# Transposed probabilities in a new packing, and a landing buffer two transfers deep

## The reference

```
q = x_norm @ wq ; k, v = x_norm @ wkv          # 32 heads, 128 columns each
scores = q @ k.T * scale, masked to k <= q     # 1024 x 1024 per head
probs  = softmax(scores)
attn   = probs @ v ; x = x + attn @ wo
```

## Time and profile before

| what | value |
|---|---|
| median of three runs | 1215.86 us |
| span of the profiled execution, first to last instruction | 1215.2 us |
| TensorE matmul busy | 1186.3 us, 98% of the span, 6400 matmuls |
| VectorE busy | 863.2 us, 71% |
| ScalarE busy | 820.0 us, 67%, 1527 instructions |
| GpSimd busy | 316.7 us, 26% |
| placing (line 533) | 384 instructions, 305.6 us |
| transposing transfers | 256, median 3.3 us from issue to landing |

### The profile page before, as it was taken

The page is one execution under the profiler, slowest core; times in us unless marked ns, Lnnn a source line. Parts: engine busy times, 40 slices in busy tenths (PEclk is TensorE's granted clock), DMA queues, the critical chain, the costliest instruction groups (busy, mean ns, idle before and its releaser), DMA issues.

```text
span 1215.2 us, 20757 instructions
## 1 busy us (share of the span) xinstructions
PE 1186.3 (98%) x6400; PEld 1036.9 (85%) x6400; DVE 863.2 (71%) x1490; ACT 820.0 (67%) x1527; POOL 316.7 (26%) x281
## 2 busy tenths in 40 slices
PE   4999999999999999999999999999999999999798
PEld 3888889888888988888898988889898888988677
DVE  7566776777677677667767676776767677777873
ACT  2576767676676667667667757766776776767753
POOL 3323122313322231322223132223313222230300
PEclk9999999999999999999999999999999999999999
DMA  3354435444443545444345444434453453454401
GB/s 121 70 112 103 98 79 108 93 102 98 97 104 73 106 99 105 98 95 104 71 101 109 98 95 99 104 78 94 106 106 86 101 110 81 87 105 96 102 1 70
DMA packets 354549, 114.34 MB, mean 94 GB/s; under 512 B 305888, under 2 KB 348384, under 8 KB 354528
## 3 DMA queue, kind: packets, MB, share of 16 engines
q1 hardware_dynamic: 354528, 114.08, 44.4%
HBM read 36.44 MB, written 2.10 MB: 32 GB/s over the span
## 4 chain that ended last, share of the span: by engine, by line
PE 95%; DVE 2%; DMA 1%; ACT 1%; issue 0%; SPq 0%; DVEq 0%; ACTq 0%
PE psC L781 61%; PE psC L833 17%; PE psS L781 16%; DMA pt<-p 1%; DVE p L709 0%; DMA res<-in_L_attn_hidden_states 0%; DVE probs L633 0%; PE psS L794 0%; ACT pT L533 0%; DVE xT L639 0%; DVE res L668 0%; ACT probs L515 0%; DVE stats L609 0%; ACT p L524 0%; DVE qkT L734 0%
## 5 line engine op out<-in xcount | busy, mean ns | idle before, releaser
L781 PE MATMUL psC<-xT,wqk 128*128 128x512 f32 x1536 | 372.2, 391 | 1.7 <-DVE xT L639 1.7
L781 PEld LDWEIGHTS psC<-xT,wqk 128*128 128x128 f32 x1536 | 286.1, 189 | 60.8 <-DVE xT L639 2.1
L533 ACT ACTIVATE pT<-pt 128x1024 fp32r<-128x1024 f16 (+3 forms) x384 | 305.6, 841 | 2.4 <-DMA pt<-p 2.4
L781 PE MATMUL psS<-qkT 128*128 128x512 f32 (+2 forms) x1152 | 245.5, 342 | 1.1 <-ACT probs L515 1.1
L709 DVE SCALAR_TENSOR_TENSOR p<-probs,p 128x128 f16<-128x128 f32 (+7 forms) x256 | 221.2, 869 | 16.1 <-ACT p L524 16.0
L703 DVE TENSOR_TENSOR psS<-psS,mask 128x128 f32<-128x128 f32 x256 | 75.7, 296 | 220.5 <-PE psS L781 219.9
L668 DVE SCALAR_TENSOR_TENSOR res<-psC,rinv,res 128x512 f32<-128x512 f32 x256 | 186.4, 743 | 61.4 <-PE psC L781 54.7
L833 PE MATMUL psC<-pT,v 128*128 128x512 f32 (+2 forms) x1152 | 221.2, 346 | 1.9 <-DVE res L668 1.1
L833 PEld LDWEIGHTS psC<-pT,v 128*128 128x128 f32 x1152 | 196.5, 188 | 30.4 <-DVE res L668 2.7
L781 PEld LDWEIGHTS psS<-qkT 128*128 128x128 f32 x1152 | 198.4, 189 | 27.8 <-ACT probs L515 1.6
L515 ACT ACTIVATE probs<-psS,negmax 128x128 f32<-128x128 f32 (+7 forms) x256 | 189.2, 739 | 44.3 <-DVE negmax L705 43.6
(11 more groups left out here) (55 smaller groups left out, 611.9 us busy)
## 6 DMA issues: line engine op xcount, KB each, us to landing
raw<-in_L_attn_wkv SPq DMA_DIRECT2D x64, 256.0 KB, 3.9
raw<-in_L_attn_wq SPq DMA_DIRECT2D x32, 256.0 KB, 3.1
raw<-in_L_attn_wo SPq DMA_DIRECT2D x32, 256.0 KB, 4.4
pt<-p SPq DMA_TRANSPOSE x256, 3.3
res<-in_L_attn_hidden_states SPq DMA_DIRECT2D x8, 256.0 KB, 6.0
out<-res SPq DMA_DIRECT2D x8, 256.0 KB, 2.0
raw<-in_L_ffn_k SPq DMA_DIRECT2D x3, 256.0 KB, 3.6
scl<-in_L_ffn_s SPq DMA_DIRECT2D x3, 0.5 KB, 5.1
```

Source lines behind the costliest of these rows:

```text
L533: last = nc.scalar.activation(pT[:, :, places, :], src[:, :, first_kt:first_kt + m, :], ACT.Copy, scale=1.0 / UP)
L781: last = nc.tensor.matmul(out_ap, w, x, start=(k == 0), stop=(k == len(terms) - 1))
```

## The change

The places of `pT` get a new formula, `pt16` shrinks from 26 to 15 places, placing is one instruction for every tile, and SP gets a wait. Blocks of tiles i >= 4 stand in rows of four (stride 4 from kt to kt+1); blocks of tiles i < 4 stand in the places that such rows leave unused, with stride -5. The zero block moves from place 15 to place 0.

```
 def block_at(kt, i):
-    return 7 * kt + i if kt < 4 else 13 + 3 * kt + i
-ZERO_AT = 15
-PLACES = block_at(7, 7) + 1
-def sections(i): ...
+    return 1 + 4 * kt + i - 4 if i >= 4 else 33 - 5 * kt + i
+ZERO_AT = 0
+PLACES = block_at(0, 3) + 1
+def places_of(i):
+    if i >= 4:
+        return slice(block_at(0, i), block_at(i, i) + 1, 4)
+    return slice(block_at(0, i), block_at(i, i) - 1, -5)
...
-        pt16 = sb("pt16", [P, 26, 2 * P], F16)
+        pt16 = sb("pt16", [P, 15, 2 * P], F16)
...
         def turned_blocks(n):
-            at = (0, 5, 11, 18)[n % 4]
+            at = (0, 7)[n % 2]
...
                     if step == "l":
+                        if not isinstance(g, int) or count(g, j, 8, n - 1) > 0:
+                            sp.wait_ge(placed, count(g, j, 8, n - 1))
+                            sp.sem_inc(turn_go, 1)
                         sp.wait_ge(p_lo, count(g, j, 8, n + 1))
                         sp.sem_inc(turn_go, 1)
                         sp.dma_start_transpose(turned_blocks(n), ...)
...
             def place(g, j, n):
-                for first_kt, m, places in sections(n):
-                    last = nc.scalar.activation(pT[:, :, places, :], src[:, :, first_kt:first_kt + m, :],
-                                                ACT.Copy, scale=1.0 / UP)
-                last.then_inc(placed, 1)
+                nc.scalar.activation(pT[:, :, places_of(n), :], src, ACT.Copy, scale=1.0 / UP).then_inc(placed, 1)
...
-    nc = _bacc.Bacc("TRN2", target_bir_lowering=False, num_devices=1)
+    nc = _bacc.Bacc("TRN2", target_bir_lowering=False, num_devices=1, dynamic_dma_scratch_size=1024)
```

More of the change, by code:

```diff
@@ L165, in block_at @@
 def block_at(kt, i):
-    return 7 * kt + i if kt < 4 else 13 + 3 * kt + i
-ZERO_AT = 15
-PLACES = block_at(7, 7) + 1
-def sections(i):
-    m = min(i, 3) + 1
-    out = [(0, m, slice(block_at(0, i), block_at(m - 1, i) + 1, 7))]
+    return 1 + 4 * kt + i - 4 if i >= 4 else 33 - 5 * kt + i
+ZERO_AT = 0
+PLACES = block_at(0, 3) + 1
+def places_of(i):
     if i >= 4:
-        out.append((4, i - 3, slice(block_at(4, i), block_at(i, i) + 1, 3)))
-    return out
+        return slice(block_at(0, i), block_at(i, i) + 1, 4)
+    return slice(block_at(0, i), block_at(i, i) - 1, -5)
 def build(nc, hidden, wq, wkv, wo, k0, s0, k1, s1, k2, s2, out):
```

## The result

| | median of the runs | lowest to highest |
|---|---|---|
| before | 1215.78 us | 1215.49 to 1216.01 (4 runs) |
| after | 1221.63 us | 1220.32 to 1224.62 (4 runs) |

The ratio is 1.0047, 95% interval 1.0035 to 1.0060: the changed kernel is slower by 5.9 us, where +2.5 was forecast and 1220.6 was the upper end of the range. Its profiled execution took 1222.37 us with a span of 1220.5. The run stands 1.9 us over its span here and 0.8 before; in every later comparison the kernel before has 1.8 too, and so has the change without the smaller scratch, so this difference belongs to the measuring and not to the change.

A forecast was written before the change was run, and what follows sets the result against it. TensorE was taken to bound the kernel (matmuls in flight 98% of the span). Loop 0, first group +2.0 and end of attention +0.5 gave +2.5 us, span 1217.7, plus 0.7 to the runs' median: 1218.4 us, range 1215.9 to 1220.6.

The forecast's parts named there:

- Placing in one instruction, 0: All heads: 128 fewer ScalarE instructions save 12.8 us of ScalarE's work, worth 0 behind a busy TensorE.
- places of pT, 0: TensorE's matmuls: the wider gap to the zero block costs 0, bounds -1 and +1 us.
- 280: Sign, whole kernel: placing falls to 256 instructions and about 280 us busy.
- The rival that ScalarE is the bound: Whole kernel: 12.8 us less ScalarE work releases something, 1213 us or less; chance 0.04.
- The loop, 0: 14 passes: ScalarE waits about 2.2 us per pass at c1@1, slack before s6@1 hides it; 0 us.
- First group, +2.0: First group: later transfers 3 and 4 delay chains v5 by 1.05 and v6 by 0.9 us; bounds 0 and 3.8.
- 4.9 us behind the loads: First group: transfer 3, issued behind the weight loads, takes 4.9 us to land.
- pays twice: Rival, first group: transfer 4 lands after 5.1 us, v6 is 1.8 us later, 1220.2 us; chance 0.12.
- End of attention, +0.5: End of attention: +0.2 from transfer 7 of the last head, 0.3 from GpSimd beside VectorE; bounds 0.1 and 1.
- The 0.2 for transfer 7@1: End of attention: waiting for c5@1 sends it about 0.3 us later, c7@1 in one piece gives 0.1 back.
- two regions are enough everywhere: Rival, first group: TensorE absorbs the shift, leaving +0.4, 1216.3 us, not slower; chance 0.14.
- stalling loop: Rival, loop: e4@1 is late for s6@1, each microsecond over the slack costs 14 us; chance 0.10.

The follow-up runs named there:

- layout: New places and one-instruction placing, but four landing regions, no wait and the default scratch: 1216.07 us, 1.0002 against the kernel before.
- scratch: Kernel before with only the smaller scratch of the DMA rings: 1216.14 us against 1215.72, ratio 1.0001.
- wait loop: Changed kernel with four landing regions, default scratch, and the wait in the 14 loop passes alone: 1215.76 us, 0.9998 against before.
- Loop later: The kernel of "wait loop", with transfer 1@1 also waiting for chain o1@0 in every loop pass: 1231.14 us, 1.0123 against before.
- the two with fill: Seven unread matmuls ahead of v5 in the first group, default scratch: added to the change 1220.63 us, 1.0035; added to "wait first" 1219.72 us, 1.0025.
- Loads late: Changed kernel with default scratch, the first head's four weight loads behind transfer 3 instead of transfer 2: 1218.38 us, 1.0022 against before.
- wait last: Changed kernel with four landing regions, default scratch, and the wait in the last group and end of attention alone: 1218.08 us, 1.0013 against before.
- default scratch: Changed kernel without the smaller scratch of the DMA rings: 1221.08 us, 1.0048 against before.
- two deep: Two landing regions and the wait, but old places, two instructions for tiles 4 to 7, and default scratch: 1221.14 us, 1.0048 against before.
- wait third: Changed kernel with four landing regions, default scratch, and a wait for the place of tile n-3 instead of n-2: 1216.05 us, 1.0005 against before.
- wait first: Changed kernel with four landing regions, default scratch, wait in the first group alone: 1220.57 us, 1.0034 against before; again 1218.50 us, 1.0017.

## Why the prediction was wrong, step by step

- *Placing in one instruction, 0; places of pT, 0; scratch, 0.* Right, each by itself: "layout" and "scratch" lie 0.35 and 0.42 us from before, inside their intervals. (The gap to the zero block was 9 places in chain 0 and 26 in chain 1; the prediction read only the 9.) The instruction itself was right too (1916 ns, 295.7 us in all; 280 was written as 305.6 less 128 x 0.197, which should have used the 0.1 us that two in a row overlap, 292.8). The rival that ScalarE is the bound is refuted by "layout".
- *The loop, 0.* Right: 1014.12 and 1014.13 us, and "wait loop" is at 0.9998. ScalarE waits at c1@1 as worked out (2.35 us for some 2.2), in the pass of the earlier trace rows:

```profile
647.15 0.63 ACT L532 ACTIVATE pT<-pt 128x512 fp32r<-128x512 f16 x1 [2.35 <-DMA pt<-p]
```

  The slack was put down to s6@1 with 2.3 us; in after it is 2.0, and o2@0, through qk2@2's evacuation, has one of 2.2 beside it. "Loop later" went past both. The cover is as thin as said: past it each delay costs 14 passes.
- *First group, +2.0.* The mechanism was right: SP waits, the loads and transfer 3 go later, h5@0 and v2 with them, v5 and v6 lack a bank. The term was too small. It moved transfer 3 by 2.1 us, rightly (54.3 worked out, 54.2 measured), and kept its landing at the 4.9 of the one row there was the earlier trace rows. In the eight traces where it stands in the old position it lands after 4.8 to 5.5 us, all at no cost; in the seven where it stands in the new one after 5.0 to 6.5, and v2's release passes each tenth to v5 in full. The stretch costs +2.64 in the best trace, +3.2 in the two with fill, +3.6 to +4.5 in four others, and on medians +4.4 and +1.75 in two comparisons of the same kernel, whose intervals (2.7 to 5.6 and 1.0 to 3.3) meet at about 3. The step that failed is "4.9 us behind the loads": a single landing behind 1 MB of loads was used as if it were a constant. Of after's 3.63, 1.95 was in the sum, 0.8 is the landing (5.7 for 4.9), 0.5 the way from the landing to v4's evacuation (24.7 us by the count above, 24.2 in the prediction; 0.2 of it is transfer 4, 3.5 for 3.3), and 0.4 the lower clock. I had put the long landing on transfer 4 (the rival "pays twice") where it came on transfer 3. "Loads late" shows the same from the other side: with transfer 3 ahead of the loads it goes to +0.59. Why one execution needs 5.0 and another 6.5 stays open.
- *End of attention, +0.5.* Too small by 1.4: the trace has +1.9, and the medians of "wait last" +1.9 (0.5 to 2.7). The term priced transfer 7@1 and the GpSimd neighbour, and the step that failed here is that it left out that the walk of the loop's head 1 (c7@0, transfer 1@1, c1@1, e4@1) happens in the last group too, where TensorE already waited 1.13 us for pv0@1's bank and so has no slack. There c1@1 waited 3.50 us, not 2.2, since the transfer took 3.6 to land instead of 2.4:

```profile
1136.85 0.63 ACT L532 ACTIVATE pT<-pt 128x512 fp32r<-128x512 f16 x1 [3.50 <-DMA pt<-p]
```

  Everything from h4@1 on is later. VectorE of after at l4@1, the residual step and the first mask of s6@1:

```profile
1140.45 0.85 DVE L706 SCALAR_TENSOR_TENSOR p<-probs,p 128x640 f16<-128x640 f32 x1 [1.07 <-ACT p L524]
1141.23 0.74 DVE L665 SCALAR_TENSOR_TENSOR res<-psC,rinv,res 128x512 f32<-128x512 f32 x1
...
1142.49 0.28 DVE L700 TENSOR_TENSOR psS<-psS,mask 128x128 f32<-128x128 f32 x1
```

  The mask stands at 1138.12 in before: 4.37 later, 0.91 more than the 3.46 that after brings into the group. pv0@1 gets +0.89 (+1.11 to +2.27 in the five other kernels with this wait, where c1@1 waits 3.80 to 4.05). It and the `o` chain then run at 0.64 of the clock (3.15 and 2.18 us for 2.21 and 1.55), and GpSimd's last weights, which wait for that `o`, give part back, their subtraction being shorter (why is not shown). GpSimd of after and of before:

```profile
1153.40 1.27 POOL L403 TENSOR_TENSOR wos<-raw,wos 128x512 fp32r<-128x512 f32 x1
```

```profile
1147.47 2.13 POOL L403 TENSOR_TENSOR wos<-raw,wos 128x512 fp32r<-128x512 f32 x1
```

  How much of the +1.01 behind pv0@1 belongs to the wait is not shown, as said under the table. The 0.2 for transfer 7@1 was right where it was worked out: c7@1 ends 8.25 us behind the end of h7@1, where it was 8.02. But it no longer comes last. What the `o` chain ahead of the feed-forward net waits for is VectorE, which is in the layer norm until then; in before it had idled for the copy of pv1@1:

```profile
1166.00 0.67 DVE L651 TENSOR_TENSOR attn<-psC,attn 128x512 fp32r<-128x512 f32 x1
```
- *From span to time.* The 0.7 us between span and run came from the first measuring of before; it is 1.8 in every comparison since. It does not explain the miss: before's medians are 1215.7 to 1216.8 with either, and where both sides have 1.8 ("default scratch", "two deep") the loss is still 5.4 us, so of the 3.2 by which 1221.63 misses 1218.4 at most some 0.5 can come from it.

By the trace of after the sum is 0 + 3.6 + 1.9 where it was 0 + 2.0 + 0.5. The rival "two regions are enough everywhere" is refuted by "two deep". It went with the rule to double-buffer in the Trainium skill, "Trainium Kernel Development and Optimization", Best Practices: here two regions overlap transfer and compute and still cost 5.4 us. The loss wherever a wait is near, which the prediction drew from early issue and late wait (the Trainium skill, "DMA: Bandwidth & Descriptors", Rules for kernel authors), is borne out: an earlier issue takes it away in "loads late" (first group) and "wait third". The "stalling loop" did not come; "loop later" priced it.

The clock was in no term. In the first group it falls behind each of the four waits of 1.85 us and more and stays at 1.00 behind 1.13. At pv0@1 it falls behind four of the six waits of 1.86 to 1.89 us and stays at 1.00 behind two ("default scratch", "loads late"), so the length of the wait does not decide it alone; what does is open. In the first group it costs 1.3 us of slower matmuls and 0.4 on balance.

## What to carry to other kernels

A landing buffer is deep enough when the consumer's own order never lags its depth: count in the order lists how many places lie between a transfer's issue and the release that it would wait for (a wait three places back cost nothing that the runs can tell, two places back 5 us), in the unrolled first and last group as well as in the loop. A wait put into a queue delays all that stands behind it, and if bulk loads stand there, the next small transfer pays for them too; let it pass the loads, or give small tiles private places. A landing time behind bulk loads is a range, so take the upper end for any wait that TensorE sees, and walk the same chain again through each stage that has idle time already.

## What the runs showed of the hardware

- Behind a wait of 1.85 to 2.64 us of an otherwise full TensorE in the first group the granted clock of the next 4 us is 0.57 to 0.62 (four traces), behind 1.13 us it is 1.00. Seven matmuls in the gap keep it at 1.00 (two traces). But behind a wait of 1.86 or 1.87 us at pv0@1 the next 3 us have 1.00 in two traces and 0.56 to 0.74 in four, and behind the same wait of 3.50 us near the end they have 0.57 in before (4 us) and 1.00 in "wait first".
- A transposing transfer of tile 3 (four blocks, high and low half) behind four loads of 256 KB lands after 4.8 to 6.5 us in 15 traces; ahead of them it took 3.1, and then the next one, behind them, 5.5.
- The chain of 12 matmuls behind a short wait of TensorE, at full clock, takes 1.69 or 1.70 us where it else takes 1.59 or 1.60 (default scratch, loads late and both fills); v5 right behind the seven filling matmuls takes 1.69 too.
